# Banded attention with its window loop written out: maxima as extra rows of the query stack, two score products issued in turn

## What is computed

```python
H, DH, HALF = 16, 8, 64
scale = DH ** -0.5
qkv = x @ Wqkv + bqkv
q, k, v = heads(...)                          # 16 heads of 8 numbers
scores = einsum('bhid,bhjd->bhij', q, k) * scale
scores = where(abs(i - j) <= HALF, scores, neg)
attn = softmax(scores)
out = einsum('bhij,bhjd->bhid', attn, v)
return out.reshape(b, n, d) @ Wout + bout
```

## Time and profile before

| | |
|---|---|
| median of 3 runs | 861.48 us (861.15 to 864.0) |
| profiled execution, its own time | 861.29 us |
| its span | 859.5 us |
| granted TensorE clock, mean | 0.904 |
| busy PE / DVE / ACT / POOL | 660.1 / 525.7 / 344.9 / 359.2 us |
| attention, first instruction to the next layer's first transfer | 291.9 us |

### The profile page before, as it was taken

One profiled execution on the slowest core, in us unless ns is written; L12 is line 12 of the kernel. 1 busy time (PEld: TensorE's weight loads), 2 busy tenths in 40 slices (PEclk: granted clock), 3 DMA queues, 4 the chain that ended last, 5 costly groups with the idle time before them and its releaser, 6 DMA issues. The chain is left out here.

```text
span 859.5 us, 18332 instructions
## 1 busy us (share of the span) xinstructions
PE 660.1 (77%) x7554; PEld 384.0 (45%) x7554; DVE 525.7 (61%) x1094; ACT 344.9 (40%) x522; POOL 359.2 (42%) x330
## 2 busy tenths in 40 slices
PE   0617888888888279976977498058998988999995
PEld 0302444444445179876876234023333344444442
DVE  8647667676664733342413667869999974406266
ACT  1421433444344573242414552346544536434320
POOL 9202444444444300000001253228999974966530
PEclk9967999999999559997977689669999999999998
DMA  3156552000000364000000640000000000000000
GB/s 76 37 107 108 89 72 32 0 0 0 0 0 2 111 199 100 3 4 2 4 4 5 261 112 0 0 1 0 0 1 0 0 1 1 1 0 1 12 13 25
DMA packets 17327, 29.76 MB, mean 35 GB/s; under 512 B 3248, under 2 KB 13168, under 8 KB 16240
## 3 DMA queue, kind: packets, MB, share of 16 engines
q1 hardware_dynamic: 17264, 28.87, 14.1%
HBM read 24.54 MB, written 4.19 MB: 33 GB/s over the span
## 5 line engine op out<-in xcount | busy, mean ns | idle before, releaser
L474 ACT ACTIVATE pr_exp<-at_psum 128x1024 f32<-128x1024 f32 x68 | 69.6, 1023 | 131.9 <-PE at_psum L559 131.9
L366 DVE TENSOR_REDUCE pr_neg_max<-at_psum 128x4 f32<-128x1024 f32 x68 | 83.2, 1225 | 49.8 <-PE at_psum L541 49.8
L316 POOL TENSOR_SCALAR_AFFINE_SELECT pr_exp<-pr_exp 128x512 f32<-128x512 f32 x68 | 47.1, 692 | 159.0 <-ACT pr_exp L474 159.0
L1493 POOL TENSOR_TENSOR all_phi_b<-all_phi_b,mo_work 128x512 f32<-128x512 f32 x56 | 71.1, 1269 | 43.3 <-ACT mo_work L1699 38.6
L749 POOL TENSOR_TENSOR all_x<-all_x,ff_x_blocks 128x512 f32<-128x512 f32 x3 | 3.8, 1263 | 173.0 <-ACT ff_x_blocks L940 173.0
L1514 PE MATMUL all_psum<-all_phi,mo_xt 128*128 128x512 f32 x128 | 67.1, 651 | 7.3 <-ACT mo_work L1681 5.6
L536 PE MATMUL at_psum<-band_mask,all_ident_bf 128*128 128x512 bf16 x136 | 43.1, 400 | 38.3 <-DVE pr_q_window L359 38.3
L1463 POOL TENSOR_TENSOR mo_work<-mo_work,mo_max 128x1024 f32<-128x1024 f32 x32 | 61.3, 1916 | 22.1 <-DVE mo_max L1755 22.1
L1547 PE MATMUL all_psum<-mo_xt,all_phi_centred 128*128 128x512 f32 x128 | 65.4, 591 | 0.0
L1600 PE MATMUL all_psum<-mo_work,mo_y_slots 128*128 128x512 f32 x128 | 62.5, 595 | 1.8 <-DVE mo_work L1803 1.8
L1699 ACT ACTIVATE mo_work<-all_psum 128x512 f32<-128x512 f32 x64 | 37.7, 601 | 60.6 <-PE all_psum L1547 60.6
(11 more groups left out here) (339 smaller groups left out, 1340.2 us busy)
## 6 DMA issues: line engine op xcount, KB each, us to landing
all_expert_w<-in_expert_w SPq DMA_DIRECT2D x1, 4096.0 KB, 18.3
ff_b_up<-in_b_up SPq DMA_DIRECT2D x1, 2048.0 KB, 10.2
ff_a_up<-in_a_up SPq DMA_DIRECT2D x1, 2048.0 KB, 16.1
ff_w_down<-in_w_down SPq DMA_DIRECT2D x2, 1024.0 KB, 20.5
at_q_stack<-parts_scratch SPq DMA_DIRECT2D x24, 64.0 KB
at_k_stack<-parts_scratch SPq DMA_DIRECT2D x24, 64.0 KB
at_q_stack<-parts_scratch SPq DMA_DIRECT2D x12, 128.0 KB
at_k_stack<-parts_scratch SPq DMA_DIRECT2D x12, 128.0 KB
```

Of the source, the lines that this page charges most:

```text
L316: nc.gpsimd.affine_select(out=e[:, g, :, 0, :], in_=e[:, g, :, 0, :], compare_op=ALU.is_ge, fill=0.0, base=0, pattern=[[0, GH], [-1, P]], ...
L366: nc.vector.tensor_reduce(negm[:, GH * g:GH * g + GH].rearrange("p (u r) -> p r u", r=2), psum[:, SN + 2 * (g % 2):SN + 2 * (g % 2) + 2, : ...
L474: nc.scalar.activation(e[:, g, :, :, :].rearrange("p h j q -> p (h j q)"), psum[:, ST:ST + 2, :].rearrange("p b n -> p (b n)"), ACT.Exp).t ...
L1493: nc.gpsimd.tensor_tensor(tot[:, ch % 2, :], first, ec[:, ch % 2, j, :], ALU.add).then_inc(added, 1)
```

## The change

The whole of `attention` is written anew.

- Q and K parts go straight from where they are made into the stacks, without DRAM, a kind of part at a time; the stacks' flag row and three rows of ones are filled by six transfers. x is loaded and normalised in three groups of tiles.
- The negated maxima, in three bf16 parts, are transposed and sent by two small transfers a window into three rows of the query stack, beside rows of ones in the key stack. The transposed product then contains them, and the selecting products are gone. The factor `scale` moves into the exponential.
- A window has eight units m of two heads. The natural product is taken in four strips of 32 queries against 160 keys, and the mask is one product of 320 columns. DVE reduces 128 x 320 a unit, ACT exponentiates 128 x 512.
- The loop is unrolled, the products read the stacks without window copies, natural scores run two windows ahead. In `scores` a transposed product in one row half is followed by two natural strips in the other, four times a unit.
- The projection is made tile by tile within the loop, its bias as a product with a row of ones; layer norm of the first twelve tiles is done in the last two windows. 16 products of identity by identity stand ahead of the first naturals and 16 ahead of the loop (`keep_warm`).

```diff
-TERMS_Q, TERMS_K = "hhmmhl", "hmhmlh"
+    NW = NT + 1
+    NU = 8
+    QC, WIN = 32, 160
+    FLAG, PARTS = 48, 49
+    TERMS_Q, TERMS_K = "hhhmml", "hmlhmh"
...
+                def stack(group, kind):
+                    r0, r1 = STACKS[group]
+                    sp.wait_ge({"h": hi_ready, "m": mid_ready, "l": low_ready}[kind], 2 * r1 // 512)
...
+                                    sp.dma_start(dst[p0:p0 + DH, :, pad + r0:pad + r1], part[k][64 * half:64 * half + 64, which, r0:r1]).then_inc(stacked[group], 16)
...
+                    v.tensor_reduce(nm[:, r, 0, j:j + 2], psum[:, SN + n % 3, 0:2 * WIN].rearrange("p (i k) -> p i k", i=2), AX_X, ALU.max, negate=True).then_inc(sn_free, 1)
...
+                def take_maxima(w):
+                    act.wait_ge(mt_done, w + 1)
...
+                        act.dma_start(qs[p0:p0 + 3, :, w * P:w * P + P], m_t[24 * half:24 * half + 24, w % 2, :]).then_inc(nm_in[w % 2], 16)
...
+                def open_natural(w, m):
+                    n = nat_unit(w, m)
...
+                    slot_free(pe, n)
+                    nc.tensor.matmul(psum[:, SN + n % 3, 0:2 * WIN].rearrange("p (i k) -> p i k", i=2), c["identb"][:, :], mask[:, :].unsqueeze(1).broadcast_to([P, 2, WIN]), start=True, stop=False)
...
+                def natural(w, m, i, q):
+                    n = nat_unit(w, m)
+                    r, j = head(other(m), i)
+                    rows = slice(64 * r, 64 * r + PARTS)
+                    k0 = w * P + q
+                    return nc.tensor.matmul(psum[q:q + QC, SN + n % 3, WIN * i:WIN * i + WIN], qs[rows, j, k0:k0 + QC], ks[rows, j, k0:k0 + WIN], start=False, stop=(i == 1))
...
+                def transposed(w, m, i, b):
+                    n = NU * w + m
+                    r, j = head(m, i)
+                    rows = slice(64 * r, 64 * r + PARTS + 3)
+                    return nc.tensor.matmul(psum[:, ST + n % 3, 256 * i + P * b:256 * i + P * b + P], ks[rows, j, (w + b) * P:(w + b) * P + P], qs[rows, j, w * P:w * P + P], start=True, stop=True)
...
+                def scores(s, m):
+
+                    open_transposed(s, m)
+                    if s + 2 < NW:
+                        open_natural(s + 2, m)
+                    for i in range(2):
+                        for b in range(2):
+                            t = transposed(s, m, i, b)
+                            if s + 2 < NW:
+                                natural(s + 2, m, i, 2 * b * QC)
+                                n = natural(s + 2, m, i, 2 * b * QC + QC)
+                    t.then_inc(st_done, 1)
+                    if s + 2 < NW:
+                        n.then_inc(sn_done, 1)
...
+                for s in range(NW):
+                    for m in range(NU):
+                        scores(s, m)
+                        if m == 0 and s >= 1:
+                            values(s - 1, 2)
+                        if m == 1 and s >= 1 and s + 1 < NW:
+                            maxima_t(s + 1)
+                        if m == 1 and s >= 3:
+                            project(s - 3)
+                        if m == 2 and s >= 1:
+                            values(s - 1, 3)
+                        if m == 4 and s >= 1:
                             values_nat(s - 1)
+                        if m == 4:
+                            values(s, 0)
+                        if m == 6 and s >= 1:
                             attn_t(s - 1)
+                        if m == 6:
+                            values(s, 1)
```

More of the change, by code:

```diff
@@ new lines, in attention @@
+        bout = a.sb("bout", [1, P])
+        bias = a.sb("bias_row", [1, P])
+        one = a.sb("one_row", [1, P])
+        xn = a.sb("xn", [P, NT, P])
+        y = xn
+        xt = a.sb("xt", [P, T])
+        rest = a.sb("rest", [P, 2, 2, 512])
+        part = {k: a.sb(f"part_{k}", [P, 2, T], BF16) for k in "hml"}
+        ones = a.sb("ones", [3, (NT + 2) * P], BF16)
+        flags = a.sb("flags", [1, (NT + 2) * P], BF16)
+        mask = a.sb("mask", [P, WIN], BF16)
+        nm = a.sb("neg_max", [P, 2, 3, NP])
@@ new lines, in attention, with nat_unit @@
+        nm_in = [a.sem(f"nm_in_{k}") for k in range(2)]
+        st_done, exp_done, sel_done, pv_done, o_ready, on_done, rec_ready, norm_done, at_done, at_ready, y_ready = (a.sem(k) for k in (
+            "st_psum", "exp_done", "sel_done", "pv_psum", "values_sbuf", "values_psum", "rec_ready", "norm_done", "at_psum", "at_ready", "y_ready"))
+        misc_bf = psum[0:3 * H, MISC, 0:64].bitcast(BF16)
+        head = lambda m, i: (m % 2, 2 * (m // 2) + i)
+        other = lambda m: m ^ 1
+        def nat_unit(w, m):
+            s = w - 2
+            return NU * w + m + max(0, s - 3) + (1 if s >= 3 and m >= 2 else 0)
@@ new lines, in _ @@
+                pe.wait_ge(ident_loaded, 16)
+                transposes(0)
+                pe.wait_ge(qk_loaded, 32)
+                project_qk(0)
+                transposes(1)
+                project_v(0)
+                project_qk(1)
+                for ch in range(2, NCH):
+                    transposes(ch)
+                    project_v(ch - 1)
+                    project_qk(ch)
+                project_v(NCH - 1)
+                pe.wait_ge(out_loaded, 48)
+                pe.wait_ge(v_ready, NCH)
@@ new lines, in _ @@
+                nc.tensor.matmul(psum[0:1, 7, 0:P], bv[:, 0:1], wout[:, :], start=True, stop=True).then_inc(bias_done, 1)
+                pe.wait_ge(xt_ready, NCH)
+                pe.wait_ge(rest_ready, 2 * NCH)
+                pe.wait_ge(consts, 10)
+                keep_warm(WARM)
+                pe.wait_ge(pads, 1)
+                pe.wait_ge(rows_in, 96)
+                pe.wait_ge(bias_ready, 1)
+                pe.wait_ge(pv_zeroed, 1)
+                for w in range(2):
+                    for m in range(NU):
+                        naturals(w, m)
+                    maxima_t(w)
```

803 lines of the change are left out of this document (381 added, 422 removed).

## The result

The changed kernel takes **1027.7 us** (median of 4 runs, 1022.01 to 1028.34) against 861.3 for the kernel before in the same session (859.39 to 864.0): 1.1915 times as long, with a 95% interval of 1.187 to 1.196. The profiled execution is the one of 1022.01 us, with a span of 1020.3. The forecast was 881, with a range of 765 to 900: the direction is right, the size is not, and the time is that of rival B, "about 1020", which had a chance of 0.04.

The account below looks back on a forecast made before the run. The prediction took TensorE's stream, with its tile-shape changes, as the bound. Against 861.3 us it summed +48 for the loop, −23 for the start and −5 for the tail to 881 us, range 765 to 900.

Parts of the forecast that it names:

- rival B: Granted clock falls to its lower level in the loop: window 25 us, about 1020 us in all; chance 0.04.
- Term (4): TensorE's order in the loop: nine shape changes a unit, 1.51 us a unit, 15.8 us a window, loop +48 us.
- Term (5): Start before the loop: stacking straight from SBUF lets the loop begin at 50 us (46 to 58), not 73.2: −23.
- up to 5: Window 8's wait for the last third of the stacks: up to 5 us if windows took under 9, otherwise nothing.
- Term (6): Tail, last value product to next layer: most tiles normalised earlier, 10.5 us for 15.5, −5.
- its own case: The forecast's main case, bounded by 0.09 to 0.12 us a shape change and start 46 to 58: 863 to 905 us.
- DVE's reduction: DVE in the loop: reduces 320 elements a unit, not 1024, at 0.49 us each, not bounding the window.
- ACT's exponential: ACT in the loop: eight exponentials of 512 elements a window at 0.58 us each, not bounding the window.
- the change of shape as the bound: TensorE in the loop: nine tile-shape changes a unit at 0.10 us each, 0.90 of the unit's 1.51 us.
- rival A: Shape changes between disjoint row halves are free: window 8.6 to 8.9 us, 778 us in all; chance 0.33.
- Rival C: A shape change costs 0.09 us, window 14.9, start at 42, tail −6: 858 to 864 us; chance 0.09.
- sign of error: What would show the forecast wrong: a window under 12 us, or a granted clock under 0.9 in the loop.

Follow-up runs that it names:

- wide kernel: Changed kernel with the natural product in one piece of 128 queries by 256 keys instead of four strips, mask 512 columns: 833.5 us, ratio 0.970.
- e3_same_half: Changed kernel with the natural strips in the same row half as the unit's transposed products instead of the opposite one: 1026.9 us, ratio 1.192.
- grouped kernel: Changed kernel with each unit's four transposed products together, then its eight natural strips together, three shape changes a unit for nine: 911.3 us, ratio 1.057.
- f1_drains: Wide kernel with mask and natural product each cut in four, so the tile shape changes eight times a unit with no narrow strip: 966.0 us, ratio 1.127.
- g1_wide_same_half: Wide kernel with the natural products in the same row half as the unit's transposed ones, so nothing runs side by side: 928.5 us, ratio 1.084.
- g2_grouped_fill1: Grouped kernel with one useless full-array product of 512 columns at the head of each unit: 843.0 us, ratio 0.984.
- h1_alternating_fill4: Changed kernel, order untouched, with four useless full-array products of 512 columns at the head of each unit: 1014.4 us, ratio 1.179.

## Why the prediction was wrong

**The step that failed is the weighing of rival B**, in the words "Against it: in the loop now the level is the higher throughout". The old loop's level says nothing of the new loop's products. The old loop has mask and selecting products on the whole array and its score products in both halves at once; the new one has neither selecting products nor products side by side. Most of the rest followed from this one number: the mechanism, its place and its time, about 1020, stood in the text with a chance of 0.04. The trace of before held a hint that the forecast didn't weigh. In its expert layer, TensorE is recorded busy for 9.45 of 10.30 us and is granted 0.50 all through; the second fence has the groups of that stretch (busy us, mean ns, idle before):

```profile
438.50:448.80 10.30, 9.45 (x372) 8.62 (x372) 1.79 (x12) 2.15 (x4) 0.00 (x0) 0.50 0.02 5
```

```profile
L1079 PE MATMUL ff_psum<-ff_b_taken,ff_h 64*64 64x64 f32 x112 | 4.9, 351 | 1.6 <-issue 1.6
L1094 PE MATMUL ff_psum<-ff_a_taken,ff_a_up 64*32 64x32 f32 x256 | 4.1, 238 | 0.7 <-issue 0.7
```

Small tiles of two shapes, at half the clock with the engine mostly recorded busy. It is a hint and no proof: TensorE stood idle for 1.6 us just before this stretch, and the changed kernel's loop had no wait before its fall.

The Trainium skill (TensorE: Matmul & The Clock Gate, HAM oscillation) gives as the rule that TensorE must have no long idle gaps. Here it had none and lost the level: 80.00 busy of 80 us at 0.50. The measurement decides. Waits matter beside it: three kernels above lost the level in a single wait of 1.4 to 3.4 us.

**Where the 140.7 us between forecast and profiled execution (881.3 and 1022.0) lie**, term by term:

- The level, in the fifteen windows with naturals: they took 361.9 us (58.28 to 420.13). With the level forced by fillers they took 346.8, of which 15 x 6.8 are the fillers': 244.6. So 117.3 us are the level's, an estimate from these two traces.
- Term (4) at its own level: 244.6 for 237, +7.6. A unit is 1.56 for 1.51: with 0.61 of columns, each of the nine changes costs 0.105, between the bounds 0.09 and 0.12. At the lower level the unit of 2.23 has 1.23 of columns, and a change costs 0.11, not the 0.14 that rival B took from the earlier trace rows. The last two windows: 21.9 us (420.13 to 442.04) for 14, +7.9. They too run mostly at the lower level (mean granted clock 0.66).
- Term (5), the start: 58.3 for 50, +8.3. The timeline shows where:

```profile
15.86 3.46 SPq L273 DMA_DIRECT2D at_q_stack<-at_part_h  x1
...
35.66 3.63 PE L540 MATMUL at_psum<-all_ident_bf 128*128 128x512 bf16 x16
39.14 0.30 PE L575 MATMUL at_psum<-at_mask,all_ident_bf 128*128 128x320 bf16 x1
...
44.13 0.30 PE L635 MATMUL at_psum<-all_ident_bf,at_neg_max 128*48 128x128 bf16 x1 [1.02 <-DVE at_neg_max L355]
44.37 0.45 PE L575 MATMUL at_psum<-at_mask,all_ident_bf 128*128 128x320 bf16 x1
...
51.81 6.41 PE L540 MATMUL at_psum<-all_ident_bf 128*128 128x512 bf16 x16
```

  The parts left at 15.9 us (16 in the forecast) and the first naturals began at 39.1 (37). From 44.4 on the level was down already, after 4 us of narrow strips in blocks and a wait of 1 us for DVE: the second eight units took 0.77 us each for 0.49, the second warming 6.41 for 3.63. That is 5 of the 8.3 us, again the level's. The rest are the 2.1 us of the stack and two waits of 1 us for DVE's parts of the maxima, where the forecast had one hand-over of 1 us. The other thirds never stopped the alternating loop; in the wide kernel, TensorE waited 6.1 us for two transfers of maxima (L575 behind `at_neg_max_t`) while the last third was being stacked, which I had at "up to 5" for another reason; those are the waits behind which the level was down.
- Term (6), the tail: 11.4 us (442.04 to 453.47) for 10.5, +0.9. The other layers: −0.8.

Together 117.3 + 7.6 + 7.9 + 8.3 + 0.9 − 0.8 = 141.2, against 140.7, with the rest in rounding and in what lies around the span. One sum of the forecast is off in itself: a change at 0.12 adds 15 x 9 x 8 x 0.02 = 22 us and a start at 58 adds 8, so the upper end of its own case is at least 911 us, not 905. It changes nothing of the outcome.

**Right** were: DVE's reduction (0.49 us, measured 489 ns), ACT's exponential (0.58, measured 598), both hidden; the change of shape as the bound, its price at the higher level, and rival A's fall: opposite halves overlap at one shape and not between two, shown by the unchanged 24.73 us of `e3_same_half` (at the lower level; the first units of both kernels, at the higher one, take about 1.56 us as well) and by the starts side by side in the wide kernel. By the rule of the Trainium skill (TensorEngine Tiling (Array Packing), Key Properties) that the forecast weighed, a change of mode drains TensorE; the same row half for the opposite one, at no change in time, agrees with it. Rival C, 858 to 864, is out: the window is over 14.9 us at either level. The sign of error that the forecast named, a granted clock under 0.9 in the loop, is the one that came.

## What to carry to other kernels

Before TensorE's work is cut in smaller tiles, or put in an order in which the shape changes often, don't take a busy engine for one at its higher level; read the granted clock of each stage. Here the lower level cost 117 us, and the alternating order by itself 88 at the higher level (an estimate: 15 windows of 16.6 us for 10.7, the grouped kernel's 12.41 less eight fillers). Look also at where the level fell. In the grouped kernel it fell in one wait of 2 us early in the loop and stayed down for the next 230 us, so a short wait may cost far more than its length; no run without the wait shows how much. Keep one tile shape through both halves and let the hardware pair them; that took the same kernel from 1028 to 833 us, and to 810 with two waits and a warming stretch removed. To find out whether a slow stretch is the clock's, add useless full-array products: if the kernel gets faster, it is. If it doesn't, nothing is settled: one filler a unit left the alternating kernel at 0.50, four held it at 1.00.

## What the runs showed of the hardware

- A TensorE recorded busy throughout can be granted its lower level, 1.2 GHz, for 370 us on end. From the wide kernel, eight changes of shape a unit for two lost the level 5 us into the loop, with no wait (`f1_drains`). With one row half at a time (`g1_wide_same_half`) it held for 19 us, was at 0.50 after a wait of 3.4 us and did not come back in the loop's steady part, while the wide kernel came back after waits of 1.9 and 4.2 us.
- Work added brought the level back after a wait in one kernel (`g2_grouped_fill1`, 1.00 from 95 us on) and kept it from falling in another (`h1_alternating_fill4`). That the level goes by how much of the array works over the time agrees with all runs in their steady part, but no run shows how much is enough. Whether narrow tiles as such count, apart from the shape that keeps them from running beside others, was not separated.
- A change of tile shape costs nearly the same time at both levels, 0.105 and 0.11 us, while columns double (0.053 and 0.107 us for 128).
- Among products of one shape, a later one in a free row half starts before earlier ones that queue for the other half (120.77 against 120.82 us, issued fifth and second). The Trainium skill (TensorE: Matmul & The Clock Gate, Architectural detail) has the queue pull weight loads ahead of running products; the rows show products themselves out of order.
- Between the two shapes of this loop, 64x128 and 64x32 tiles, nothing overlaps, in opposite halves no more than in the same: 1026.9 us against 1027.7.
